# Half 0's layer-norm statistics move behind the projection loop, the feed-forward weights come in 2 MB pieces, and Bm moves to At's buffer

## The reference

```
x = inputs                                        # (4, 2048, 4096) f32
# attention branch
c = conv1d(x, conv_w, width 3, SAME) + conv_b     # 4096 -> 3072, split into q, k, v of 1024
qh, kh, vh = q @ wq + bq, k @ wk + bk, v @ wv + bv  # 16 heads of 64
o = softmax(causal(qh * kh / 8)) @ vh             # in blocks of 128 tokens
a = (o @ wo + bo) @ proj_w + proj_b               # 1024 -> 1024 -> 4096
x1 = layernorm(x + a)
# feed-forward branch
h = x1 @ A.T                                      # 4096 -> 16 experts x 16 = 256
f = x1 @ W.T + b + (h * probs) @ B                # 4096 -> 4096, plus 256 -> 4096
out = layernorm(x1 + f)
```

## Time and profile before

| what | us |
|---|---|
| median of 2 runs | 2476.06 (2473.02 to 2479.09) |
| profiled execution, its own time | 2474.76 |
| its span on the slowest core (core 0) | 2473.2 |
| spans of the 8 cores | 2456.8 to 2473.2 |
| PE busy (matmul) | 1890.8 |
| ACT busy | 301.9 |
| DVE busy | 228.6 |
| POOL busy | 418.8 |
| mean granted TensorE clock, 8 cores | 0.929 to 0.935 |

### The profile page before, as it was taken

How to read it: one execution, slowest core, us unless ns; L and a number is a source line. 1 busy time by engine, 2 the same in 40 slices (tenths; PEclk the granted TensorE clock), 3 DMA queues, 4 the chain that set the end, 5 groups by cost and what they waited for, 6 DMA issues and landing times.

```text
span 2473.2 us, 20035 instructions; the slowest of 8 cores (2456.8 to 2473.2 us)
## 1 busy us (share of the span) xinstructions
PE 1890.8 (76%) x8591; PEld 835.5 (34%) x8762; DVE 228.6 (9%) x162; ACT 301.9 (12%) x413; POOL 418.8 (17%) x360
## 2 busy tenths in 40 slices
PE   0399999999999999999545565542988888888810
PEld 0144444444444444444322222211433333333300
DVE  0000000000000000000421011006000000000078
ACT  0000000000000000002265232220011111111110
POOL 1112121212121212100001111116001000010068
PEclk9999999999999999999678898986999999999955
DMA  9979999898989897910215555570755665556424
GB/s 147 93 65 81 85 80 87 79 87 78 88 77 89 72 83 69 84 29 8 34 22 73 76 84 78 77 102 0 68 51 53 57 61 52 51 53 58 43 111 161
DMA packets 481611, 176.11 MB, mean 71 GB/s; under 512 B 432883, under 2 KB 465779, under 8 KB 481268
## 3 DMA queue, kind: packets, MB, share of 16 engines
q0 software_dynamic: 470720, 157.32, 63.1%
q1 hardware_dynamic: 10804, 17.50, 2.0%
HBM read 315.32 MB, written 16.78 MB: 134 GB/s over the span
## 4 chain that ended last, share of the span: by engine, by line
PE 72%; ACT 7%; DMA 7%; POOL 6%; issue 6%; DVE 2%; another core or an unknown queue 0%; ACTq 0%; POOLq 0%; DVEq 0%; SPq 0%
PE psA L333 20%; PE psB L333 20%; PE psA L972 18%; DMA xjb<-xT 5%; PE psA L763 3%; POOL ob L1061 2%; POOL ob L1057 2%; ACT sqtmp L1004 2%; PE psA L897 1%; PE psA L390 1%; PE psA L683 1%; PE psB L390 1%; PE psA L980 1%; PE psB L1021 1%; ACT sqtmp L799 1%
## 5 line engine op out<-in xcount | busy, mean ns | idle before, releaser
L333 PE MATMUL psA<-xb,cwb 128*128 128x512 bf16 x2258 | 499.0, 380 | 102.4 <-DMA cwb<-cw 99.9
L333 PE MATMUL psB<-xb,cwb 128*128 128x512 bf16 x2258 | 496.6, 378 | 2.5
L333 PEld LDWEIGHTS psA<-xb,cwb 128*128 128x128 bf16 x2304 | 223.7, 97 | 376.5 <-issue 103.2
L333 PEld LDWEIGHTS psB<-xb,cwb 128*128 128x128 bf16 x2304 | 223.2, 97 | 274.9
L296 POOL DMA_DIRECT2D cwb<-cw x144 | 164.8, 1175 | 844.5 <-PE psA L333 415.9
L972 PE MATMUL psA<-x1bA,wsA 128*128 128x512 bf16 x503 | 112.4, 379 | 1.6 <-DVE hb L907 1.1
L972 PE MATMUL psA<-x1bA,wsB 128*128 128x512 bf16 x501 | 112.5, 379 | 0.6
L1021 PE MATMUL psB<-sqtmp,ones_s 128*128 128x512 bf16 x62 | 23.3, 376 | 89.0 <-ACT sqtmp L1004 88.7
L763 PE MATMUL psA<-a1b,wsA 128*128 128x512 bf16 x250 | 73.0, 440 | 11.6 <-DMA xjb<-xT 8.5
L947 POOL DMA_DIRECT2D wsA<-Wt x16 | 26.9, 1679 | 275.2 <-PE psB L1021 244.6
L739 POOL DMA_DIRECT2D xjb<-xT x64 | 34.2, 534 | 230.9 <-PE psA L772 216.2
(11 more groups left out here) (166 smaller groups left out, 1412.9 us busy)
## 6 DMA issues: line engine op xcount, KB each, us to landing
cwb<-cw POOLq DMA_DIRECT2D x144, 512.0 KB, 22.6
wsA<-Wt POOLq DMA_DIRECT2D x16, 1024.0 KB, 11.9
wsB<-Wt POOLq DMA_DIRECT2D x16, 1024.0 KB, 12.0
outT<-ob SPq DMA_DIRECT2D x64, 256.0 KB, 2.1
xb<-xT POOLq DMA_DIRECT2D x4, 2052.0 KB, 45.3
wsA<-projw POOLq DMA_DIRECT2D x8, 1024.0 KB, 9.6
wsB<-projw POOLq DMA_DIRECT2D x8, 1024.0 KB, 10.4
xjb<-xT POOLq DMA_DIRECT2D x64, 128.0 KB, 4.9
```

The source lines that it names most:

```text
L333: return e.matmul(pbank(bank), buf[:, (w * 32 + dc) * 128:(w * 32 + dc + 1) * 128], xb[:, dc * (T + 2) + tokc * 512 + w: dc * (T + 2) + to ...
```

## The change

- **Half 0's statistics.** `emit_p4(0)` emits no statistics in its loop. After tile 31 a loop of its own appends 32 squares (ACT) and 64 matmuls (PE), with the sums in banks 0 and 1. The tiles of half 0 now use banks 0 to 3 in turn.
- **Half 1's statistics** stay in the loop, with a lag of four tiles in place of three.
- **Wt** comes in 16 pieces of 2 MB (256 columns) into wsF0 and wsF1 in place of 32 pieces of 1 MB. Two chunks of output features share a piece, and the loop runs piece, half, chunk. The lag of the statistics is four tiles in place of three.
- **Bm** lies where At lies (OFF_LINV), since wsF1 takes its old place. It is loaded when the last matmul of `emit_ht(1)` has read At; `emit_ht(0)` now waits for At alone.

The core of the diff:

```diff
-    Bmb = sb("Bmb", REG1 + 16384, (128, 2 * D), BF16)
+    Bmb = sb("Bmb", OFF_LINV, (128, 2 * D), BF16)
+    wsF0 = sb("wsF0", REG1, (128, 8192), BF16)
+    wsF1 = sb("wsF1", REG1 + 16384, (128, 8192), BF16)
...
-            bank = dmc % 2 if half == 0 else tile_i % 4
+            bank = tile_i % 4
...
-            pend_stats.append((dmc, c_evac))
-            if dmc >= 3:
-                emit_stats(*pend_stats.pop(0))
-            if dmc == DC - 1:
-                while pend_stats:
-                    emit_stats(*pend_stats.pop(0))
+            if half == 1:
+                pend_stats.append(dmc)
+                if len(pend_stats) > 4:
+                    emit_ln1_stat(pend_stats.pop(0))
+        if half == 1:
+            while pend_stats:
+                emit_ln1_stat(pend_stats.pop(0))
...
+            return
+        b1, b2 = (0, 1) if half == 0 else (4, 5)
...
+        for dmc in range(DC):
+            def sq(e, dmc=dmc):
...
+            sqw = [("cC", res1_evac[dmc])]
+            if dmc >= 2:
+                sqw.append(("tC", mm2_done[dmc - 2]))
+            S.op("scalar", sq, wait=sqw)
...
-        S.op("gpsimd", bmdma, wait=[p4_t_end], inc="w2", k=16)
-    g_at = g_bm = ("w2", S.n("w2"))
+    g_at = ("w2", S.n("w2"))
     emit_ht(0)
+    hb_done_h0 = ("vC", S.n("vC"))
     emit_ln1_apply(1)
...
+    t_p4done = ("tC", S.n("tC"))
+    wt_first_gate = [t_p4done]
     emit_wt_load(0)
     emit_wt_load(1)
     emit_ht(1)
+    t_ht_end = ("tC", S.n("tC"))
     hb_done = ("vC", S.n("vC"))
...
+        S.op("gpsimd", bmdma2, wait=[t_ht_end], inc="w2", k=16)
+    g_bm = ("w2", S.n("w2"))
...
-    for oc in range(DC):
-        par = oc % 2
-        buf = wsA if par == 0 else wsB
+    for pg in range(16):
+        par = pg % 2
+        buf = wsF0 if par == 0 else wsF1
         for half in range(2):
-            waits = [wt_ld[oc], g_bm, hb_done]
+            for sub in range(2):
+                oc = pg * 2 + sub
+                waits = [wt_ld[pg], g_bm,
+                         hb_done_h0 if half == 0 else hb_done]
...
-            if len(pend_stats2) > 3:
+                if len(pend_stats2) > 4:
```

More of the change, by code:

```diff
@@ new lines, in emit_p4, with sq, mm1, mm2 @@
+        b1, b2 = (0, 1) if half == 0 else (4, 5)
+        stat_w1 = [bank_free[b1]] if b1 in bank_free else []
+        stat_w2 = [bank_free[b2]] if b2 in bank_free else []
+        for dmc in range(DC):
+            def sq(e, dmc=dmc):
+                return e.activation(
+                    sqtmp[:, (dmc % 2) * 512:(dmc % 2) * 512 + 512],
+                    res1_ap(dmc), AF.Square)
+            sqw = [("cC", res1_evac[dmc])]
+            if dmc >= 2:
+                sqw.append(("tC", mm2_done[dmc - 2]))
+            S.op("scalar", sq, wait=sqw)
+            c_sq = S.n("cC")
+            def mm1(e, dmc=dmc, b1=b1):
+                return e.matmul(pbank(b1), ones128[:, :], res1_ap(dmc),
+                                start=(dmc == 0), stop=(dmc == DC - 1),
+                                skip_group_check=True)
+            S.op("tensor", mm1,
+                 wait=stat_w1 + [("cC", res1_evac[dmc])],
+                 inc="tC" if dmc == DC - 1 else None)
+            stat_w1 = []
+            def mm2(e, dmc=dmc, b2=b2):
+                return e.matmul(pbank(b2), ones128[:, :],
+                                sqtmp[:, (dmc % 2) * 512:
+                                      (dmc % 2) * 512 + 512],
+                                start=(dmc == 0), stop=(dmc == DC - 1),
+                                skip_group_check=True)
+            S.op("tensor", mm2, wait=stat_w2 + [("cC", c_sq)], inc="tC")
+            stat_w2 = []
+            mm2_done.append(S.n("tC"))
@@ L953, in build_nc, with bmdma2 @@
     emit_ht(1)
+    t_ht_end = ("tC", S.n("tC"))
     hb_done = ("vC", S.n("vC"))
+    for erc in range(ERC):
+        def bmdma2(e, erc=erc):
+            return e.dma_start(
+                out=Bmb[:, erc * D:(erc + 1) * D],
+                in_=Bm[erc * 128:(erc + 1) * 128, :])
+        S.op("gpsimd", bmdma2, wait=[t_ht_end], inc="w2", k=16)
+    g_bm = ("w2", S.n("w2"))
     ln2 = {0: dict(b1=4, b2=5, mm2_done=[]), 1: dict(b1=6, b2=7, mm2_done=[])}
@@ new lines, in build_nc, with emit_stats2, sq2, mm1 @@
+    res2_writes = {}
+    def emit_stats2(oc, half, c_evac):
+        hs = ln2[half]
+        def sq2(e, oc=oc, half=half):
+            return e.activation(
+                sqtmp[:, half * 512:half * 512 + 512],
+                res2_ap(oc)[:, half * TH:half * TH + TH], AF.Square)
+        sqw = [("cC", c_evac)]
+        if oc >= 1:
+            sqw.append(("tC", hs["mm2_done"][oc - 1]))
+        S.op("scalar", sq2, wait=sqw)
+        c_sq = S.n("cC")
+        def mm1(e, oc=oc, half=half, b1=hs["b1"]):
+            return e.matmul(
+                pbank(b1), ones128[:, :],
+                res2_ap(oc)[:, half * TH:half * TH + TH],
+                start=(oc == 0), stop=(oc == DC - 1),
+                skip_group_check=True)
+        S.op("tensor", mm1, wait=hs["w"][hs["b1"]] + [("cC", c_evac)],
+             inc="tC" if oc == DC - 1 else None)
+        hs["w"][hs["b1"]] = []
+        def mm2(e, oc=oc, half=half, b2=hs["b2"]):
+            return e.matmul(
+                pbank(b2), ones128[:, :],
+                sqtmp[:, half * 512:half * 512 + 512],
+                start=(oc == 0), stop=(oc == DC - 1),
+                skip_group_check=True)
+        S.op("tensor", mm2, wait=hs["w"][hs["b2"]] + [("cC", c_sq)],
+             inc="tC")
+        hs["w"][hs["b2"]] = []
+        hs["mm2_done"].append(S.n("tC"))
```

182 lines of the change are left out of this document (76 added, 106 removed).

## The result

The changed kernel takes 2492.71 us (median of 12 runs) against 2477.73 for the kernel before on the same chips: ratio 1.0063, 95% interval [1.0052, 1.0074], or 15.6 us slower. The forecast was 12.2 us slower than the profiled execution, 2487.0. In some executions of any of these kernels the cores of one die show a lower granted clock and end later; the ratios leave these out, but two of the four executions behind e5's ratio, at 2400.48 and 2402.83 us, are a little of that kind (two cores at 0.915 to 0.917).

What follows compares the result with a forecast made beforehand. PE was taken as the bound in convolution and feed-forward, with chains of waits between. Terms -9.6 + 0.7 - 10.2 + 28.4 + 2.6 + 0.2 = +12.1 on 2474.8 gave 2487.0 us, range 2464 to 2509.

Steps and rivals of the forecast that it cites:

- At: Low-rank product: its first matmul, released by At without Bm, starts 10.2 us earlier (-8 to -12).
- the entrance: Start of feed-forward: Bm queues behind two 2 MB Wt loads, so the first matmul comes 28.4 us later (+16.8 to +36).
- (a): Rival at the feed-forward entrance: Wt runs at Bm's pace, so 28.4 becomes 16.8; 2467 to 2475 us; chance 0.25.
- (b): Rival in half 0's tail: squares and sums alternate, 48 us instead of 25, 2510; chance 0.2 together with rival (d).
- (c): Rival in feed-forward: loads bind the stage, +98 us, 2585; chance 0.05 including other things beyond 2%.
- The loop of half 0: Output projection of half 0: without statistics, five groups save 21.5 us and the stretch after the last load 12.4.
- rival (d): Half 0 gains only about 15 us instead of 33.9, as x and projw land later; 2506; chance 0.2 with (b).
- The tail: After half 0's loop: 32 squares and 64 matmuls take 25 us, at least 23; net +22.0 with evacuation and end.
- The bank wait: Half 1's first wo tile waits for ACT to read the sums in bank 0: +2.3 us.
- the sum by the rule: Feed-forward entrance under the 512 B rule: wide Wt loads run at Bm's pace, giving the lower bound, +16.8 us.
- Feed-forward and slow clock: Feed-forward stage: low clock after PE's idle adds 2.6 us, the lag of four tiles a net 0.2.

Runs made afterwards that it cites:

- e5: Kernel before, with ACT in the feed-forward stage squaring the tile of three tiles ago before evacuating the newest: 2400.48 us, ratio 0.964.
- e9: Kernel before, with half 0's statistics behind the loop and its low-rank product waiting for At alone, Bm in its old buffer: 2453.13 us, ratio 0.9896.
- e3: Changed kernel, with POOL issuing Bm ahead of the second Wt piece instead of behind it: 2476.37 us, ratio 0.9998 of the kernel before.
- e4: Changed kernel, with half 0's sums in banks 2 and 3 instead of 0 and 1: 2487.82 us, ratio 1.0045 of the kernel before.
- e1: Kernel before, with half 0's low-rank product waiting for At alone and Bm on its own semaphore in its old buffer: 2464.33 us, ratio 0.9955.
- e8: Changed kernel, with each 2 MB Wt piece loaded by two loads of 128 columns: 2503.75 us, ratio 1.0101 of the kernel before.
- e2: Kernel before, with half 0's statistics emitted only after tile 31, banks unchanged: 2466.93 us, ratio 0.9965.
- e6: Kernel before, with squares ahead of the newest tile's evacuation in both output projections only: 2433.29 us, ratio 0.9823.
- e7: Kernel before, with squares ahead of evacuations in both projections and feed-forward, and the low-rank product waiting for At alone: 2324.52 us, ratio 0.9378.
- e10: The version of e7, with the x load issued ahead of the projw load: 2320.47 us, ratio 0.9363 of the kernel before.
- e11: Changed kernel, with Bm ahead of the second Wt piece and half 0's sums in banks 2 and 3: 2471.56 us, ratio 0.9971 of the kernel before.

## Why the prediction was right

**The sign and the mechanism held.** The forecast said: half 0 and At win about 20 us, and the entrance gives back more, since Bm stands behind 4 MB of Wt. e9 shows the first half of this (26 us won without the entrance), e3 the second (16 us come back by moving Bm ahead of one piece). No rival was needed for the result: (a) falls, since the entrance took 49.4 us on the mean of the cores and not 34; (b) falls, since 32 squares ran without a gap; (c) falls, since no feed-forward matmul waits for Wt after the first tile. What (a) had for it, that the x loads ahead of At may have made its 19.0 longer, falls too: they stand there in the changed kernel as before, and At lands in 15.3 to 17.2.

That the sum came so close is in part luck. By the table the terms were off by +3.6, +1.7, -3.9, +0.3, +3.9 and -0.4 us, and the -3.9 of At cancelled the +3.9 of the entrance.

**The sizes, term by term.**

- *The loop of half 0*, forecast -33.9: the sums end 8.3 us earlier after a tail that is 20.4 longer (24.8 from tile 31's last matmul to the last sum, 4.4 before), so the loop gave -28.7. The forecast had 5 too much. By the issues of the projw loads (mean of the cores) the five groups gave 19.3 of their 21.5 and the stretch behind the last load 9.6 of its 12.4. x was late next, as rival (d) said, though at a price of at most 5 us and not of 19. PE's waits for x grew from 20.9 to 43.2 us in this half, but part of that growth was in the forecast, since a shorter tile begins to wait for the same landing earlier. How much of the 5 us is x was not separated.
- *The tail*, forecast 25: squares at 0.72 us a pair to the end. On core 2 the clock was at its upper level throughout; on cores 0, 1 and 3 eight of the sums' matmuls, over 3 us, ran at the lower one, which ACT's pace hid in part. The lower bound, 23, was the right one. The timeline of core 2:

```profile
1430.86 5.68 ACT L842 ACTIVATE sqtmp<-res1lo 128x512 bf16<-128x512 bf16 x8
...
1436.62 17.21 ACT L842 ACTIVATE sqtmp<-res1hi 128x512 bf16<-128x512 bf16 x24
```

- *The bank wait*, forecast +2.3: the idle was 2.27 on every core. The term left out the slow clock behind it, 1.2 us on the mean; the kernel before has 0.6 of slow clock in the same matmuls, so 0.6 is new. With the pair at the end of half 1, +0.7, this is 3.6 of the +4.7 measured; the rest stays open.
- *At*, forecast -10.2 (-8 to -12): -13.4 from issue to first matmul. The missing 3 us are At's own landing, 15.3 to 17.2 us on the eight cores instead of the 19.0 of core 0. The 19.0 was not a property of the load: the kernel before had 15.6 to 19.6 on its eight cores. The bound -12 was too tight, because I had put At's landing as fixed.
- *The entrance*, forecast +28.4 within +16.8 to +36: +32.3 on the mean. The second Wt piece cost 16.3 (49.4 less e3's 33.1), as forecast (16), though no row had shown the 3 us of start taken off there. The missing 3.9 lie in the first piece and Bm, forecast at 29.5 and 33.1 in e3: there the first piece lands sooner than 19.0 (16.1 us on core 0, 17.8 on core 4), but Bm's second half only 15.3 to 16.8 us after its issue, where the forecast had 10.2 for all of Bm. Seven cores lie between 46.6 and 49.9 us from the first Wt issue to the first matmul, core 2 at 56.4, which is beyond the upper bound of 52.8. Windows of core 2 show it moving 114 and 108 GB/s (last figure) in the first 18 us of its wait:

```profile
1724.00:1733.00 9.00, 0.00 (x0) 0.00 (x0) 0.00 (x0) 0.00 (x0) 0.00 (x0) 0.51 1.13 114
1733.00:1742.00 9.00, 0.00 (x0) 0.00 (x0) 0.00 (x0) 0.00 (x0) 0.00 (x0) 0.50 1.03 108
1742.00:1752.00 10.00, 0.00 (x0) 0.00 (x0) 0.00 (x0) 0.00 (x0) 0.00 (x0) 0.50 1.00 156
```

  Why that core drew less in these 18 us stays open; it did not recur in e3, where all cores lie between 32.5 and 33.9.
- *Feed-forward and slow clock*, forecast +2.8: +2.4.

**On the 512 B rule.** At the entrance the forecast weighed the least size of 512 B for full rate that the Trainium skill gives on its page "DMA: Bandwidth & Descriptors", section "Specifications". The traces agree with it in direction: wide rows moved 116 to 166 GB/s on core 6 while Wt was loaded, narrow ones 95 to 107. The width did not bring the loads to Bm's pace, and the sum by the rule (+16.8) would have been 16 us off.

**Where the expected gain went.** On the mean of the cores 23.4 us were to be had (e9). The bank wait took 4.5 (e4), the entrance 32.3 and the slow clock behind it 2.6: +16.0 of the +16.3 measured. And the largest wait that these runs could take away, the evacuation ahead of the square on ACT, was left by the change in two of three stages and bought off in the third by a tail.

## What to carry to other kernels

Where an engine waits a short, constant time in every tile, look at the order of the other engine's list before lengthening a lag: one instruction moved ahead of another was worth 44 us in the projections and 100 in the feed-forward stage here, while one more tile of lag was worth nothing. When a buffer is moved to make room, follow its load: what must be read first, and what is ahead of it in its queue. A 2 MB load that cost next to nothing behind a layer norm (e1) cost 32 us when its place was taken by a piece twice as large, and 16 of them came back by changing the order of two calls.

## What the runs showed of the hardware that was not expected

- An idle of 2.27 us on PE was followed by the lower clock for a good part of the next 32 matmuls on six of eight cores (8.42 to 8.75 us instead of 7.07), and not on cores 1 and 7; without the idle (e4) no core had it there. On five of the cores 32 pairs of matmuls with 0.29 us of idle in each 0.72 stayed at the upper level for 24 us; on cores 0, 1 and 3 eight matmuls of them ran at the lower one.
- POOL's fourth load of 1 MB in pieces of 128 columns was issued 17 to 28 us after the third although it waited for no semaphore, on all eight cores of e8: 17 to 19 us on one core of each of the pairs 0/1, 2/3, 4/5 and 6/7, and 25 to 28 on the other. With 2 MB pieces of 256 columns, two in a row went out at once, and Bm behind them as soon as its own wait was over.
- At's landing depended on the other core of a pair. In the eight kernels in which Bm is issued 7 to 11 us behind At (the kernel before, e1, e2, e5, e6, e7, e9 and e10), At landed late, 17.8 to 19.6 us after its issue, on exactly one core of each of the pairs 0/1, 2/3, 4/5 and 6/7, each time the one that issued At later, counted from its own start; on the other it landed in 15.1 to 17.2. In the five without Bm there (the changed kernel, e3, e4, e8 and e11) all forty landings lie in 15.1 to 17.2. So the delay goes with the neighbour's Bm and not with the own one. That the two share the rate of their transfers is the likely reason, but no run tested it.
